# Attention and ternary feed-forward layer on one core: late loads issued late, SyncE's issues in the planner's table, a second home for Wo, the residual in halves

## What is computed

```python
q, k = rope(x @ Wq), rope(x @ Wk);  v = x @ Wv            # q1,q2 / k1,k2: halves of 32
a1 = softmax(q1 @ k1.T * scale + mask);  a2 = softmax(q2 @ k2.T * scale + mask)
lam = exp(sum(lq1 * lk1)) - exp(sum(lq2 * lk2)) + LAMBDA_INIT
out = groupnorm((a1 - lam * a2) @ v) * gn_w + gn_b
x = layernorm(x + (out * (1 - LAMBDA_INIT)) @ Wo)
x = layernorm(x + (silu(x @ tern(W_up).T) * (x @ tern(W_gate).T)) @ tern(W_down).T)
```

## Time and profile before

| | us |
|---|---|
| median of 3 runs | 2399.93 (2399.42 to 2401.19) |
| profiled execution | 2401.43 |
| its span, first to last instruction | 2399.5 |
| mean granted TensorE clock | 0.984 |

### The profile page before, as it was taken

The page is one execution under the profiler, slowest core; times in us unless marked ns, Lnnn a source line. Parts: engine busy times, 40 slices in busy tenths (PEclk is TensorE's granted clock), DMA queues, the critical chain, the costliest instruction groups (busy, mean ns, idle before and its releaser), DMA issues.

```text
span 2399.5 us, 41382 instructions
## 1 busy us (share of the span) xinstructions
PE 2241.2 (93%) x13602; PEld 1397.6 (58%) x13602; DVE 1797.6 (75%) x3830; ACT 1457.2 (61%) x3530; POOL 1260.2 (53%) x1907
## 2 busy tenths in 40 slices
PE   7889989889899999999999999999899999999998
PEld 4556656555556666666665666666566666644444
DVE  3587898989887878887878888887777888832343
ACT  1467756464666767777666767777667767721232
POOL 0455688888664455554544555665544445521232
PEclk9999999999999999999999999999999999999999
DMA  6766655565643131312253312222342111013000
GB/s 224 221 195 217 202 176 180 176 185 171 185 137 102 45 93 58 98 54 68 87 157 94 93 54 84 80 84 63 106 119 80 49 45 62 28 56 112 1 18 18
DMA packets 257603, 256.53 MB, mean 107 GB/s; under 512 B 31344, under 2 KB 199408, under 8 KB 255216
## 3 DMA queue, kind: packets, MB, share of 16 engines
q1 hardware_dynamic: 246016, 220.26, 30.4%
q10 hardware_dynamic: 11376, 33.63, 4.3%
HBM read 182.53 MB, written 71.30 MB: 106 GB/s over the span
## 4 chain that ended last, share of the span: by engine, by line
PE 66%; DVE 14%; issue 7%; POOL 7%; ACT 2%; DMA 2%; SPq 0%; ACTq 0%; DVEq 0%; POOLq 0%
PE F L992 15%; PE PV L934 9%; PE F L979 9%; PE F L1001 8%; PE S L917 8%; PE F L962 7%; PE F L902 6%; DVE e_long L1245 4%; DVE e_long L1326 2%; PE PV L937 2%; DVE e_short L1326 2%; POOL x_lo L1218 2%; POOL linv L1175 1%; DVE e_short L1245 1%; PE F L970 1%
## 5 line engine op out<-in xcount | busy, mean ns | idle before, releaser
L1175 POOL TENSOR_TENSOR linv<-lsum,powers 128x2 f32<-128x2 f32 x512 | 412.9, 806 | 671.1 <-ACT e_long L1053 550.7
L1053 ACT ACTIVATE e_long<-e_long,nmax 128x768 f32<-128x768 f32 (+3 forms) x512 | 504.8, 988 | 156.0 <-DVE nmax L1245 152.3
L1245 DVE CUSTOM_DVE_ANT_0 e_long<-S,mask_b 128x768 f32<-128x768 f32 (+3 forms) x512 | 512.6, 1019 | 102.0 <-PE S L917 99.1
L917 PE MATMUL S<-kstk,qstk 128*128 128x384 f32 (+5 forms) x1536 | 505.4, 421 | 52.9 <-DVE nmax L1245 41.2
L917 PEld LDWEIGHTS S<-kstk,qstk 128*128 128x128 f32 x1536 | 278.0, 194 | 190.8 <-DVE nmax L1245 76.0
L1046 ACT ACTIVATE dt_long<-F 128x512 f32<-128x512 f32 (+3 forms) x512 | 239.4, 511 | 194.6 <-PE F L902 188.5
L1326 DVE SCALAR_TENSOR_TENSOR e_long<-e_long,coef 128x1024 f32<-128x1024 f32 (+3 forms) x256 | 308.9, 1207 | 49.9 <-POOL coef L1176 49.1
L1053 ACT ACTIVATE e_short<-e_short,nmax 128x384 f32<-128x384 f32 (+3 forms) x512 | 284.0, 558 | 50.5 <-DVE nmax L1245 49.0
L962 PE MATMUL F<-xT,wr 128*128 128x512 f32 x640 | 308.6, 615 | 4.1 <-issue 1.3
L1245 DVE CUSTOM_DVE_ANT_0 e_short<-S,mask_b 128x384 f32<-128x384 f32 (+3 forms) x512 | 237.9, 486 | 52.4 <-PE S L917 49.7
L979 PE MATMUL F<-wo_sb,at_sb 128*128 128x512 f32 x512 | 240.0, 603 | 15.9 <-issue 15.9
(11 more groups left out here) (107 smaller groups left out, 3361.8 us busy)
## 6 DMA issues: line engine op xcount, KB each, us to landing
qstk<-dq SPq DMA_DIRECT2D x512, 128.0 KB, 2.8
dq<-hl SPq DMA_DIRECT2D x32, 1024.0 KB, 5.0
wr<-in_w_proj ACTq DMA_DIRECT2D x48, 512.0 KB, 4.2
kstk<-dk SPq DMA_DIRECT2D x64, 256.0 KB, 5.5
da<-ra SPq DMA_DIRECT2D x32, 512.0 KB, 3.1
at_sb<-da SPq DMA_DIRECT2D x32, 512.0 KB, 4.2
x<-in_x SPq DMA_DIRECT2D x16, 512.0 KB, 6.1
dk<-hl SPq DMA_DIRECT2D x8, 1024.0 KB, 4.9
```

The costliest lines, as they stand in the source:

```text
L917: last = nc.tensor.matmul(slot[:, h, :], qstk[:, duo % 4, 2 * r + m, :].bitcast(F32R), kstk[:, g % 2, m, h * w:(h + 1) * w].bitcast(F32R), ...
L1053: nc.scalar.activation(e, e, ACT.Exp, bias=nmax[:, u % 8:u % 8 + 1], scale=-1.0, accum_out=lsum[:, n % 4, m:m + 1]).then_inc(s_exp, 1)
L1175: link(nc.gpsimd.tensor_tensor(linv[:, a % 8, :], lsum[:, a % 4, :], mone, ALU.pow))
L1245: nc.vector.tensor_tensor_reduce(out, slot, mask, -1.0, -NEG, ALU.add, ALU.min, nmax[:, u % 8:u % 8 + 1]).then_inc(s_negmax, 1)
```

## The change

Six things change. (1) `load first` of tiles 4 to 7 waits until tile 1 has been transposed; the second w is issued after the copy of tile 0, rope after that of tile 1, lambda and `gn` after that of tile 3, all as planned items of ScalarE; DVE's sums of lambda become a planned item, and the exponential follows them. (2) The residual x of batch 0 is issued after the scores of step 100. (3) `takes` gets costs for the DMA issues of SyncE. (4) Wo of the last batch goes to a place of its own, `wo_late`, which lies on the places of `xT` and `wr` and is loaded when the last projection has been multiplied. (5) The residual x of a batch is loaded in halves, each when the four stores of that half of the batch before have landed; `s_out` becomes two semaphores. (6) In the planner and on PE, the small matmuls `mean`, `variance` and `totals` also wait for the reader of the last small one, as `values` did.

```diff
-LANDS = {..., "load first": 2.5}
+LANDS = {..., "load rope": 6.0, "load lambda": 5.0, "load first": 2.5}
@@ takes
+            "load q": 1.0, "load k": 1.9, "load first": 0.5, "load x1": 0.5, "load wo": 0.48, "load a": 0.5, "store v": 0.45,
+            "store rotated": 0.45, "store a": 0.45, "store out": 0.5, "load weight": 0.5, "load v": 0.5, "load lambda": 0.8, "lambda sums": 0.5,
@@ after
-        out = [ITEM("fill", last, PIECES[last.kind] - 1)] if a >= 2 else []
+        out = [ITEM("fill", last, PIECES[last.kind] - 1)] if a >= 2 else [ITEM("copy", X_JOBS[0])] * a
+    elif what == "load first":
+        out = [ITEM("fill", X_JOBS[1], 0)] if a >= 4 else []
+    elif what in ("load rope", "load lambda"):
+        out = [ITEM("copy", X_JOBS[1 if what == "load rope" else 3])]
+    elif what == "lambda sums":
+        out = [ITEM("load lambda")]
+    elif what == "lambda":
+        out = [ITEM("lambda sums")]
...
+            out.append(ITEM("load rope"))
...
-        out = [ITEM("fill", y_last(a - 1), 1) if a else ITEM("ternary", PREP - 1)]
+        out = [ITEM("fill", PROJECTION[-1], 1) if a == B - 1 else ITEM("fill", y_last(a - 1), 1) if a else
+               ITEM("ternary", PREP - 1)]
     elif what == "load x1":
-        out = [ITEM("store out", y_last(a - 1))] if a else []
+        out = [ITEM("store out", JOB("y", a - 1, b // 2, 1, 3)) if a else ITEM("scores", 100, 1)]
@@ STRINGS
-           [ITEM("load wo", b, c) for b in range(B) for c in range(8)],
+           [ITEM("load wo", b, c) for b in range(B - 1) for c in range(8)], [ITEM("load wo", B - 1, c) for c in range(8)],
@@ choose
-                if item.what in READER:
-                    other = ITEM("product", at["pe"][2] - 1)
-                elif item.what == "values" and small:
-                    other = ITEM(READER[small.what], small.a)
+                others = []
+                if item.what in READER and at["pe"][2]:
+                    others.append(ITEM("product", at["pe"][2] - 1))
+                if (item.what in READER or item.what == "values") and small:
+                    others.append(ITEM(READER[small.what], small.a))
@@ layer_kernel
+        with ExitStack() as once:
+            wo_late = once.enter_context(nc.sbuf_tensor("wo_late", [P, 8, D], F32))
         xT = sb("xT", [P, DC, BANK])
         wr = sb("wr", [P, 2, DC, 256])
@@ block.sync
             def load_wo(b, c):
+                if b == B - 1:
+                    if c == 0:
+                        sp.wait_ge(s_ffull, INDEX[PROJECTION[-1]] + 1)
+                    sp.dma_start(wo_late[:, c, :], wo[c * P:(c + 1) * P, :]).then_inc(s_wo_late, 16)
...
             def load_x1(b, k):
-                if k == 0 and b:
-                    sp.wait_ge(s_out, 16 * NT * b)
+                if k % 2 == 0 and b:
+                    sp.wait_ge(s_out[k // 2], 16 * 4 * b)
...
                 if what == "load first":
+                    if a >= 4:
+                        sp.wait_ge(s_ffull, INDEX[X_JOBS[1]] + 1)
@@ block.scalar
-            load_w(0)
-            act.dma_start(cs[:, :, :], rope).then_inc(s_cs, 16)
-            load_w(1)
-            act.dma_start(lamv[:, :, :, :], lams_in.rearrange("(o a) b d -> o a b d", o=1)
-                          .broadcast_to((P, 2, 2, DH))).then_inc(s_lamin, 16)
-            act.dma_start(gn_sb[:, :, :], gn).then_inc(s_gn, 16)
```

More of the change, by code:

```diff
@@ L168 @@
 LANDS = {"load q": 3.1, "load k": 5.5, "load v": 4.5, "store v": 3.9, "store rotated": 5.2, "store a": 3.5, "load a": 4.4,
-         "store out": 2.5, "load wo": 4.0, "load x1": 6.0, "load weight": 4.5, "load x": 3.7, "load w": 4.2, "load first": 2.5}
+         "store out": 2.5, "load wo": 4.0, "load x1": 6.0, "load weight": 4.5, "load x": 3.7, "load w": 4.2, "load rope": 6.0, "load lambda": 5.0, "load first": 2.5}
 def width(n):
@@ L386 @@
     "act": [[ITEM("exponent", n, m) for n, m in _maps], [ITEM("evict", n, h) for n, h in _halves],
-            [ITEM("inverses", duo) for duo in range(DUOS)], [ITEM("lambda")],
+            [ITEM("inverses", duo) for duo in range(DUOS)], [ITEM("load rope")], [ITEM("load lambda")], [ITEM("lambda")],
             *[[ITEM("copy", j) for j in OF_KIND[kind]] for kind in ("xT", "V", "x1T", "up")],
@@ L396 @@
             [ITEM(what, c) for c in range(CHUNKS) for what in ("moments", "spread", "deviation")],
-            [ITEM("minus lambda")], [ITEM("all sums"), ITEM("scales"), ITEM("constants")],
+            [ITEM("lambda sums"), ITEM("minus lambda")], [ITEM("all sums"), ITEM("scales"), ITEM("constants")],
             [ITEM("ternary", i) for i in range(PREP)]],
@@ L503, in choose @@
                     continue
[L504 to L512 removed]
+                others = []
[3 more added lines that the diff above has]
+                    others.append(ITEM(READER[small.what], small.a))
+                if any(other not in end for other in others):
+                    continue
+                r = max([r] + [end[other] for other in others])
                 if item.what == "scores" and item.a and item.b == 0:
@@ L692, in layer_kernel @@
         s_rast = [sem(f"s_rast{k}") for k in range(2)]
-        s_out = sem("s_out")
+        s_out = [sem(f"s_out{k}") for k in range(2)]
         s_const = sem("s_const")
@@ L848, in store_out @@
                 t = 4 * job.h + job.j
[L849 removed]
+                sp.dma_start(out_tiles[job.b, t], x1[:, t, :]).then_inc(s_out[job.h], 16)
             def load_weight(i, again):
@@ L888, in _ @@
                     load_weight(a % PREP, a >= PREP)
-            sp.wait_ge(s_out, 16 * NT * B)
+            for half in range(2):
+                sp.wait_ge(s_out[half], 16 * 4 * B)
         @block.tensor
@@ L974, in fill @@
                     if piece == 0:
-                        if job.i == 0:
+                        if job.i == 0 and job.b == B - 1:
+                            pe.wait_ge(s_wo_late, 16 * 8)
+                        elif job.i == 0:
                             pe.wait_ge(s_wo, 16 * 8 * (job.b + 1))
                         pe.wait_ge(s_ain[i % 2], 16 * (i // 2 + 1))
+                    w = wo_late if job.b == B - 1 else wo_sb
                     for c in range(2 * piece, 2 * piece + 2):
-                        last = nc.tensor.matmul(bank[:, :], at_sb[:, i % 2, c, :], wo_sb[:, c, :], start=c == 0, stop=c == 7)
+                        last = nc.tensor.matmul(bank[:, :], at_sb[:, i % 2, c, :], w[:, c, :], start=c == 0, stop=c == 7)
                 elif job.kind == "x1T":
@@ L1009, in _ @@
             for what, a, b in ORDER["pe"]:
-                if what in READER:
-                    if made:
+                if what in READER or what == "values":
+                    if last_small:
+                        small, c = last_small
+                        pe.wait_ge({"mean": s_rv, "variance": s_gve, "totals": s_kk}[small], c + 1)
+                    last_small = None if what == "values" else (what, a)
+                    if made and what != "values":
                         pe.wait_ge(s_pvfree, made)
-                    last_small = what, a
                 if what == "scores":
@@ L1126, in _ @@
                 elif what == "load w":
-                    if a >= 2:
-                        load_w(a)
+                    load_w(a)
+                elif what == "load rope":
+                    act.dma_start(cs[:, :, :], rope).then_inc(s_cs, 16)
+                elif what == "load lambda":
+                    act.dma_start(lamv[:, :, :, :], lams_in.rearrange("(o a) b d -> o a b d", o=1)
+                                  .broadcast_to((P, 2, 2, DH))).then_inc(s_lamin, 16)
+                    act.dma_start(gn_sb[:, :, :], gn).then_inc(s_gn, 16)
                 elif what == "lambda":
@@ L1354, in _ @@
                     nc.vector.tensor_scalar(gsm[:, 3:4], PV[:, 257:258], LN_EPS, None, ALU.add).then_inc(s_gve, 1)
+                elif what == "lambda sums":
+                    dve.wait_ge(s_lamin, 16)
+                    link(nc.vector.tensor_tensor(lamp[:, :, :], lamv[:, :, 0, :], lamv[:, :, 1, :], ALU.mult))
+                    nc.vector.tensor_reduce(lams, lamp[:, :, :], AX.X, ALU.add).then_inc(s_lam, 1)
                 elif what == "minus lambda":
```

25 lines of the change are left out of this document (7 added, 18 removed).

## The result

| | runs | median us | lowest to highest |
|---|---|---|---|
| before | 4 | 2400.05 | 2399.42 to 2401.19 |
| after | 4 | 2385.62 | 2381.47 to 2387.39 |

The ratio is 0.9937, with a 95% interval of 0.992 to 0.9954: faster by 15.1 us, or 11 to 19. Predicted were 2379.0 (2363 to 2391), 20.9 faster.

The account below looks back on a forecast made before the run. The prediction took PE's work plus its idle time as the bound. Start 6.3, boundary 3 and tail 11.6 sum to 20.9 us, so 2399.93 - 20.9 = 2379.0 us, range 2363 to 2391.

Parts of the forecast that it names:

- What bounds it: Whole kernel: PE's work plus its idle time; removing no matmul, the change can only cut the idle 158.3 us.
- Part 1, the start: First loads up to the first projection: it starts at 10.5 in place of 16.8, gain 6.3 us.
- the bound of 8.6: Start: upper bound of the gain in us, if closer transposes also raised PE's clock sooner, up to 2.3 more.
- worst case of 23.4: Start: lambda lands so late that DVE is held until 23.4, six us beyond the first empty; at most 2 on PE.
- I take nothing: Batch 0's residual x at step 100, near 477 us: 2 us of SyncE issue and 2 MB, priced at no cost.
- Part 2, to the first scores: First projection to first scores: stretch of 59.7 us stays as it is, passing the start's shift through whole.
- the bound for q going first: Before the first scores: q's store issued ahead of the k loads would win 4.1 us; counted only in the range.
- Part 3, the boundary: Mixing batches 1 and 2: true SyncE issue costs plan `wo` later; gain 3 us, bounds 0 and 7.9.
- Part 4, the tail: End of attention, batch 3's mixing: late Wo removes the 9.43 us wait and 2.2 slow restart, gain 11.6 us.
- Part 5, everything else: Newly computed order of all engines, 250 to 2110 us: zero, with 8 us to either side.
- Rival A: Whole kernel: gains as summed, with the order's noise, 2371 to 2387 us; chance 0.62.
- Rival D: Stage 300 to 600 us: scores held back for q loads make the kernel slower, 2412.7 if its loss doubles; chance 0.04.

Follow-up runs that it names:

- a2_start: before with only the start's changes (first loads, rope, lambda, batch 0's residual x at step 100) and the small matmuls' waits: 2405.01 us, ratio 1.0012.
- b2_q_store_first: after with batch 0's second load of k planned behind the first loads of q: 2376.49 us, ratio 0.9891 against before.
- a4_no_table: after without SyncE's issue costs in the planner's table, lambda's two entries kept: 2396.37 us, ratio 0.9973 against before.
- a1_table: before with only SyncE's issue costs added to the planner's table: 2414.3 us, ratio 1.0053 against before.
- a3_wo_late: before with only the last batch's Wo in a place of its own: 2392.42 us, ratio 0.9959 against before.
- c3_after_90: after with SyncE's costs in the table at nine tenths, nothing else changed: 2405.77 us, ratio 1.0018 against before.
- c2_k_x_later: after with the second k load behind the first q loads and batch 0's residual x after step 145: 2367.87 us, ratio 0.9862 against before.

## Why the prediction was right or wrong

**What bounds it.** Right. PE's idle time fell by 21.0 us and the profiled span by 19.9: 6.56 at the start, 11.7 at the tail, and 1.7 between them.

**Part 1, the start.** Right, and by its own steps: projection at 10.52 (10.5), the two `xs` tiles ahead of w. The matmuls did not speed up sooner (32 records in 15.96 us, before 16.02), so the bound of 8.6 was not reached. The prediction put the slow first ones down to the half-speed level; their durations fit that, but the profile grants 1.00 there: 6 records in the 4.5 us from 10.5 and 22 in the 9 us from 15, both at a granted clock of 1.00. What slowed them is open. Rope was to be there near 14 and is wanted at 16.3; it landed at 17.45, and the first scores moved as much as the projection (6.56 and 6.27), so the two free banks hid it. Lambda was to be there by 16; it was issued at 9.84 and took 7.8 us, so 17.6. DVE reads it at 18.66 and ScalarE's exponential stands at 19.16, and for the same reason nothing came of it. (Its worst case of 23.4 lies 7.1 us beyond the first empty bank at 16.3, not six.) Wrong in one step: the residual x at step 100, "I take nothing". I had named its 2 us of issue and its 2 MB, and looked only at the q loads behind it. What stood behind it on SyncE in a2_start was a weight tile, and that cost 11.3 us. In after a gate tile stands behind it as well and lands in 9.3 us, and no stall follows, because POOL's turn for it comes 12.5 us after the issue. That step was priced at nothing without a look at the queue, and in after it cost nothing by luck.

**Part 2, to the first scores.** Right: 59.4 us (59.7), with q's store still behind the k loads. But the bound for q going first, 4.1, was too small. b2_q_store_first won 6.5, with four k loads gone from ahead of it: 0.6 us by the earlier issue (51.56 against 52.20), and the rest because the landings get shorter, by 4.5 and 1.4 us. I had priced the place in the queue and not the transfer.

**Part 3, the boundary.** 3 us predicted. The wait went from 5.88 to 1.66, but the boundary of batches 0 and 1, which I left out, went from 0.6 to 2.83, and the first four records still took 3.75. In waits the two boundaries gained 6.5 - 4.5 = 2.0; against a4_no_table SyncE's costs gain 7.6 - 4.5 = 3.1. The orders differ in more than this, but the sign is the same on before: there these two boundaries wait 6.5 us, and 11.5 - 9.2 = 2.3 in a1_table. That issue time counts at these waits is thus shown here. By the statement that it is usually small relative to the DMA itself (the Trainium skill, DMA: Bandwidth & Descriptors, section "Issuing engines are not separate DMA queues") these 3.1 us would have been zero; the waits of these runs don't agree with it.

**Part 4, the tail.** Right: 9.43 + 2.24 = 11.7 in the trace (11.6), and -9.8 in a3_wo_late's time, with 7 to 12.5 as its interval. `wo_late` was loaded from 1591.78, some 550 us before it was wanted. The third `at_sb` was issued at 2153.06, ahead of the residual x, so there was more room than "1 to 2 us". The halves, which the prediction priced at nothing, are nothing.

**Part 5, everything else.** "Zero, with 8 us to either side" was right in the profiled execution and too narrow as a bound. In that execution attention's idle time fell by 2.3 us, which the boundaries' 2.0 nearly make up; the waits for `nmax` are 41.5 us against 41.2, and a new stall of 4.8 us, with a granted clock of 0.50 from 627 to 632 us behind it, stands against smaller gains. But the same SyncE's costs on before gave +12.7, and with every cost a tenth smaller the whole change +4.3. The order's share was between -9 and +11 us on a4_no_table, and between +13 and +20 on before.

**The sum.** 20.9 us were forecast and 15.1 measured. In the trace the named parts make 6.6 + 2.0 + 11.7 = 20.3, for a span 19.9 shorter: the parts' sizes miss by 0.6 in all, the boundary alone by 1.0, and 4.8 lie between the two profiled executions and the ratio of the medians (before's lies 1.4 above its median, after's 4.2 below), where no trace says what was lost. Rival A is what happened, and its range of 2371 to 2387 held the time. That is in part luck: the start and the tail were understood, but c3_after_90, the same change with costs a tenth away that nobody can read that exactly, came out at 2405.77, outside the whole range and slower than before. Rival D, that SyncE's costs in the table slow the stage 300 to 600, was priced at 0.04 for the whole change: that stage lost 39.4 us, inside the 26 to 42 that I had named. A chance of 0.04 for slower was too small, and its place too narrow: in c3_after_90 the stage loses 39.7, and it is 600 to 900 that loses 21.0 in place of after's 14.4. It isn't a stage with little slack but, where a cause could be named, a cluster of loads that comes to stand ahead of a store or a weight whose reader is due.

**What stays open.** The named stalls (step 100, near step 130) explain single losses of 5 to 11 us. The diffuse part, 9 to 16 us in 79 to 83 waits for `nmax` in place of 64 to 69, I can attribute to the order but not to one mechanism in it.

## What to carry to other kernels

When an order is computed from a table, price the new order as a term of its own, and size it by perturbing the table: here a tenth on SyncE's costs moved the whole by 8 and 19 us, more than most of the change's parts, and a single version's time says little about whether the costs are truer. Judge the parts with the order held, and compute the orders of the versions to see whether it is. And when a large load is moved to "some quiet time", look at what comes behind it in the same queue, and how soon its reader is due: a store or a weight tile that lands in 10 to 12.7 us in place of the usual 5 stalls engines three hand-overs away where the reader is due at once (a2_start), and nobody where it is due 12.5 us later (after). Moving two such loads, in c2_k_x_later, was worth as much as the start and the tail together.

## What the runs showed of the hardware

A transfer's time from issue to landing depended on what its queue was given just before: the first store of q took 12.43 us behind eight loads of k, and 7.97 behind four fewer; a store of q behind loads of Wo, q and k took 12.70; a weight tile behind 2 MB of residual x took 10.43 in a2_start and 9.3 in after. The page of after, part 6 (KB each, median us from issue to landing), has for all 32 stores of q:

```profile
dq<-hl SPq DMA_DIRECT2D x32, 1024.0 KB, 5.5
```

A plan with one landing time for each kind of transfer, as the planner's table has it, misses the cases that stall.

In the first 4.5 us of the first projection PE ran 6 records, and 22 in 9 us after it, while the granted clock reads 1.00 in both stretches; elsewhere such slow matmuls stand beside a granted clock of 0.50 (627 to 632 us of after). So at the start the clock's row doesn't tell the pace.

The same program spreads by more than I had taken from four runs (2399.42 to 2401.19): on other chips before ran from 2396.87 to 2408.65, and c3_after_90 from 2399.47 to 2415.0. Differences under some 5 us between single executions say nothing here; this is why the sizes above go by the ratios of medians.
